# Three fp32r terms for the up products of batches 0 to 5, centred up weights, and a new order of the tail in an RWKV and mixture-of-experts kernel

## What is computed

```python
shifted = pad(hidden)[:, :-1]                       # the token before
key, value, rec = (hidden * m + shifted * (1 - m) for m in (mix_k, mix_v, mix_r))
k, v, r = key @ Wk, value @ Wv, sigmoid(rec @ Wr)
rwkv = _wkv(time_decay, time_first, k, v)           # a scan over time with running max, numerator, denominator
x = layernorm(hidden + r * rwkv @ Wo)
gate = softmax(x @ router_w.T) * top2_mask          # 8 experts
a = silu(einsum('bth,eih->beti', x, down_w))        # 16 hidden units per expert
out = einsum('beth,bte->bth', einsum('beti,ehi->beth', a, up_w), gate)
x = layernorm(x + out)
```

## Time and profile before

| | |
|---|---|
| median of 3 runs | 495.65 us (495.41 to 495.65) |
| the profiled execution | 495.26 us, its span 493.4 us |
| mean granted TensorE clock | 0.986 of full speed |
| busy share of the span | PE 96%, PEld 64%, DVE 83%, ACT 69%, POOL 53% |
| DMA | 29.95 MB on the queue, 18.6% of the 16 engines' span |

### The profile page before, as it was taken

How to read it: one execution, slowest core, us unless ns; L and a number is a source line. 1 busy time by engine, 2 the same in 40 slices (tenths; PEclk the granted TensorE clock), 3 DMA queues, 4 the chain that set the end, 5 groups by cost and what they waited for, 6 DMA issues and landing times. The chain is left out here.

```text
span 493.4 us, 6302 instructions
## 1 busy us (share of the span) xinstructions
PE 471.9 (96%) x1850; PEld 316.4 (64%) x1850; DVE 408.8 (83%) x655; ACT 338.7 (69%) x769; POOL 259.5 (53%) x279
## 2 busy tenths in 40 slices
PE   8998799999999999999999999999999999999991
PEld 3444377777777667775777667776677656776550
DVE  6998988897799878997799977998699977776686
ACT  1568365865867678786777769776787767657574
POOL 2446764566515964457625767259635574321326
PEclk9999799999999999999999999999999999999997
DMA  9800250003000042004110032001320012300015
GB/s 248 277 12 1 86 191 1 0 3 85 1 1 0 24 147 87 1 1 129 64 64 1 1 129 106 22 1 63 107 89 1 0 43 86 128 1 1 1 38 219
DMA packets 20098, 30.35 MB, mean 62 GB/s; under 512 B 2016, under 2 KB 7136, under 8 KB 20064
## 3 DMA queue, kind: packets, MB, share of 16 engines
q1 hardware_dynamic: 20064, 29.95, 18.6%
HBM read 21.56 MB, written 8.39 MB: 61 GB/s over the span
## 5 line engine op out<-in xcount | busy, mean ns | idle before, releaser
L514 ACT ACTIVATE PR<-PR 128x512 f32<-128x512 f32 x128 | 74.3, 581 | 53.0 <-PE PR L296 23.1
L320 PE MATMUL PP<-WO,RW 128*128 128x512 f32 x216 | 97.3, 592 | 0.0
L1026 POOL TENSOR_SCALAR NM<-SUM,RS 128x1 f32<-128x1 f32 x30 | 9.1, 302 | 157.3 <-ACT RS L514 157.3
L320 PEld LDWEIGHTS PP<-WO,RW 128*128 128x128 f32 x216 | 39.5, 190 | 41.3 <-issue 40.9
L1020 POOL TENSOR_TENSOR DQ<-DEN,EX 128x512 f32<-128x512 f32 x32 | 41.0, 1282 | 35.4 <-DVE DEN L730 35.4
L767 DVE TENSOR_TENSOR RW<-NU,PR 128x512 f32<-128x512 f32 x32 | 22.0, 687 | 42.3 <-ACT PR L514 42.2
L778 DVE SCALAR_TENSOR_TENSOR KT<-D,VEC,XT 128x512 f32<-128x512 f32 x56 | 52.0, 959 | 0.0
L292 PE MATMUL PV<-VH,WVH 128*128 128x512 f32 x112 | 47.0, 420 | 0.4 <-DVE NU L754 0.4
L292 PE MATMUL PK<-KH,WKH 128*128 128x512 f32 x112 | 47.2, 422 | 0.0
L730 DVE TENSOR_TENSOR_SCAN DEN<-PK,EX 128x512 f32<-128x512 f32 x32 | 39.1, 1221 | 9.7 <-ACT EX L514 7.5
L292 PE MATMUL PR<-RH,WRH 128*128 128x512 f32 x112 | 47.0, 419 | 0.2 <-DVE RW L767 0.2
(11 more groups left out here) (200 smaller groups left out, 1119.2 us busy)
## 6 DMA issues: line engine op xcount, KB each, us to landing
XT<-in_xt SPq DMA_DIRECT2D x32, 256.0 KB, 3.6
XN<-in_x SPq DMA_DIRECT2D x28, 256.0 KB, 2.7
out<-XN SPq DMA_DIRECT2D x28, 256.0 KB, 2.0
WO<-in_wo SPq DMA_DIRECT2D x1, 1024.0 KB, 7.7
XT<-in_x SPq DMA_DIRECT2D x4, 256.0 KB, 4.1
out<-XT SPq DMA_DIRECT2D x4, 256.0 KB, 2.2
X1T<-in_wk SPq DMA_DIRECT2D x2, 256.0 KB, 4.9
XN<-in_wv SPq DMA_DIRECT2D x2, 256.0 KB, 5.3
```

The lines of the kernel that those rows point to most:

```text
L320: last = eng.matmul(projected_at(t), RW[(C * b + c) % NRW][:, 128 * n:128 * n + 128], WO[:, c, :], start=(c == 0), stop=(c == C - 1))
L514: eng.activation(*a, **k).then_inc(q[s], 1)
L1026: eng.tensor_scalar(NM1[:, col(t)], total, RS1[:, col(t)], scale, ALU.mult, ALU.mult)\
```

## The change

- UP is centred over its 512 columns once (ACT sums a row of it, POOL makes the mean and subtracts it), in slots 4 and 5. The row mean of the second residual is then zero, since its other summand is normalised. So `residual2` no longer makes a sum, `spread2` squares without a bias, `normalise2` loses its 128x1 product and `finish` its subtraction.
- UP is split into UPH and UPL (fp32r). For batches 0 to 5 `ffn_out` writes AGH (fp32r), DVE subtracts it from the turned gates in PSUM to AGL (`gated_low`, new), and `ffn_up` is three fp32r matmuls. Batches 6 and 7 stay fp32.
- SCR (4 x 512 columns) becomes JUNK (512). Batch 0's key mixes go to WO, so WO's load moves behind DR and TRI and waits for the fourth key product.
- The up product of `j = 0` goes behind the projection. In the tail the order of PE, ACT, DVE and POOL changes; MEASURED shrinks from five tiles to three, all of batch 7, FINISHED from two to one, and Ln and Exp of batch 6 are made for two tiles at a time.

```diff
@@ full @@
-                early = [AGT[:, :], UP[:, :]] + ...
-                return (SCR[:, c, :], RW[C + c][:, :], early[c])[which]
+                early = [JUNK[:, :], UP[:, :]] + ...
+                return (WO[:, c, :], RW[C + c][:, :], early[c])[which]
@@
-        MEASURED = [NT * (LAST - 2) + 3, NT * (LAST - 1) + 1, NT * (LAST - 1) + 3, NT * LAST + 1, NT * LAST + 3]
+        MEASURED = [NT * LAST + 1, NT * LAST + 2, NT * LAST + 3]
-        FINISHED = [NT * LAST + 1, NT * LAST + 3]
+        FINISHED = [NT * LAST + 3]
@@ sync @@
-            load_w(WO, wo, "wo")
             load_w(DR, dr, "dr", 0, HD)
             eng.dma_start(TRI[:, :], tri).then_inc(q["tri"], 16)
+            eng.wait_ge(q["k"], C)
+            load_w(WO, wo, "wo")
@@ tensor, ffn_up @@
+                if k < LAST - 1:
+                    eng.wait_ge(q["agl"], k + 1)
...
-                eng.matmul(up_at(t), PARTS[k].agt[:, o:o + 128], UP[:, :],
-                           start=True, stop=True).then_inc(q["up_"], 1)
+                if k < LAST - 1:
+                    eng.matmul(up_at(t), AGH[:, o:o + 128], UPH[:, :], start=True, stop=False)
+                    eng.matmul(up_at(t), AGH[:, o:o + 128], UPL[:, :], start=False, stop=False)
+                    last = eng.matmul(up_at(t), AGL[:, o:o + 128], UPH[:, :], start=False, stop=True)
+                else:
+                    last = eng.matmul(up_at(t), PARTS[k].agt[:, o:o + 128], UP[:, :], start=True, stop=True)
+                last.then_inc(q["up_"], 1)
@@ tensor, the loop @@
-                if j == 0 and batch(b - 3):
-                    ffn_up(t3 + 3)
                 if j == 0:
                     for t in now[:1]:
                         project(t)
+                if j == 0 and batch(b - 3):
+                    ffn_up(t3 + 3)
                 rec(s)
@@ tensor, the tail @@
             turn(t7)
+            ffn_turn(LAST - 1)
+            ffn_up(t5)
             project_most(t7 + 3)
             project_rest(t7 + 3)
             turn(t7 + 1)
             hidden(t7)
+            ffn_up(t5 + 1)
             turn(t7 + 2)
-            ffn_up(t5)
             hidden(t7 + 1)
-            ffn_up(t5 + 1)
+            ffn_up(t5 + 2)
             turn(t7 + 3)
             hidden(t7 + 2)
+            ffn_up(t5 + 3)
             hidden(t7 + 3)
-            ffn_turn(LAST - 1)
-            ffn_up(t5 + 2)
-            ffn_up(t5 + 3)
+            ffn_up(t6)
             ffn_turn(LAST)
-            ffn_up(t6)
@@ scalar @@
+                if s == C:
+                    eng.wait_ge(q["up"], 16)
+                    act("upx", JUNK[:, :], UP[:, :], ACT.Copy, accum_out=SUMU[:, :])
+                if s == C + 1:
+                    eng.wait_ge(q["upc"], 1)
+                    act("uph", UPH[:, :], UP[:, :], ACT.Copy)
@@ vector @@
+            def gated_low(k):
+                eng.wait_ge(q["agc"], k + 1)
+                eng.tensor_tensor(AGL[:, :], PARTS[k].turned_at, AGH[:, :].bitcast(F32), ALU.subtract)\
+                   .then_inc(q["agl"], 1)
@@ vector, the loop: behind scan_max(s + 1) and lead(s + 1), ahead of the mixes @@
+                if j == 2 and s < U - 2 and batch(b - 2):
+                    gated_low(b - 2)
                 if j == 2 and b:
                     mixes(b + 1, 1, 0, 1)
...
                 if s == U - 1:
+                    gated_low(LAST - 2)
                     gate_scores(LAST - 1)
@@ gpsimd @@
             def normalise2(t):
...
-                eng.tensor_scalar(xn_at(t), xn_at(t), RS2[:, col(t)], NM2[:, col(t)], ALU.mult, ALU.add)\
-                   .then_inc(q["nrm2"], 1)
+                eng.tensor_scalar(xn_at(t), xn_at(t), RS2[:, col(t)], None, ALU.mult).then_inc(q["nrm2"], 1)
@@
+                if s == C:
+                    eng.wait_ge(q["upx"], 1)
+                    eng.tensor_scalar(NMU[:, :], SUMU[:, :], -1.0 / H, None, ALU.mult).then_inc(q["upm"], 1)
+                    eng.wait_ge(q["upm"], 1)
+                    eng.tensor_scalar(UP[:, :], UP[:, :], NMU[:, :], None, ALU.add).then_inc(q["upc"], 1)
+                if s == C + 1:
+                    eng.wait_ge(q["uph"], 1)
+                    eng.tensor_tensor(UPL[:, :], UP[:, :], UPH[:, :].bitcast(F32), ALU.subtract).then_inc(q["upl"], 1)
```

More of the change, by code:

```diff
@@ L74, in rwkv_moe_postln @@
         ST, MV = sb("ST", [128, 7, 6]), sb("MV", [128, 7, 2])
-        SUM2, SQ2, LV2, RS2, NM2 = (sb(n + "2", [128, 3 * NT]) for n in ("SUM", "SQ", "LV", "RS", "NM"))
+        SQ2, LV2, RS2 = (sb(n + "2", [128, 3 * NT]) for n in ("SQ", "LV", "RS"))
+        SUMU, NMU = sb("SUMU", [128, 1]), sb("NMU", [128, 1])
         PK = [bank("PK0"), bank("PK1")]
@@ L113, in __init__ @@
                 tail = self.b == LAST
-                x = SCR if tail else X1T
                 hs = spare[:, 0:NT * HD].rearrange("p (n h) -> p n h", n=NT) if tail else HS[self.b % 2]
@@ L117, in __init__ @@
                 gm = spare[:, 768:780].rearrange("p (i n) -> p i n", i=3) if tail else GM
-                self.s1, self.s2 = (x[:, i, EI * lo:EI * hi] for i in range(2))
-                self.gt, self.eq = (x[:, 2 if tail else 1, o + E * E * lo:o + E * E * hi] for o in (0, 256))
+                s1, s2, pairs = (M, DEN, NUM) if tail else (X1T[:, 0, :], X1T[:, 1, :], X1T[:, 1, :])
+                self.s1, self.s2 = (a[:, EI * lo:EI * hi] for a in (s1, s2))
+                self.gt, self.eq = (pairs[:, o + E * E * lo:o + E * E * hi] for o in (0, 256))
                 self.hs = hs[:, lo:hi, :]
@@ L573, in spread, with spread2 @@
                 act("rs1", RS1[:, col(t)], LV1[:, col(t)], ACT.Exp, scale=-0.5)
-            def spread2(t):
+            def spread2(t, n=1):
+                cols = slice(col(t).start, col(t).start + n)
                 if t in MEASURED:
                     i = MEASURED.index(t)
-                    eng.wait_ge(q["mv2"], i + 1)
-                    act("lv2", LV2[:, col(t)], MV[:, i, 1:2], ACT.Ln, bias=EPS)
-                else:
[L581 to L587, removed]
+                    eng.wait_ge(q["mv2"], i + n)
+                    eng.activation(LV2[:, cols], MV[:, i:i + n, 1], ACT.Ln, bias=EPS).then_inc(q["lv2"], n)
+                else:
+                    for u in range(t, t + n):
+                        eng.wait_ge(q["res2"], u + 1)
+                        act("sq2", JUNK[:, :] if u == t else KT[0][:, :], xn_at(u), ACT.Square, accum_out=SQ2[:, col(u)])
+                    eng.wait_ge(q["sq2"], squared(t + n - 1, MEASURED))
+                    eng.activation(LV2[:, cols], SQ2[:, cols], ACT.Ln, bias=EPS, scale=1.0 / H).then_inc(q["lv2"], n)
+                eng.wait_ge(q["lv2"], t + n)
+                eng.activation(RS2[:, cols], LV2[:, cols], ACT.Exp, scale=-0.5).then_inc(q["rs2"], n)
             def turned(t):
@@ L691, in _ @@
             spread(t7 + 2)
+            ffn_out(LAST - 1)
+            spread2(t5)
             turned(t7 + 1)
@@ L696, in _ @@
             hidden_copy(t7 + 1)
-            spread2(t5)
+            ffn_in(LAST)
             turned(t7 + 3)
             hidden_copy(t7 + 2)
-            ffn_in(LAST)
+            spread2(t5 + 1)
             hidden_copy(t7 + 3)
-            ffn_out(LAST - 1)
             ffn_in(LAST + 1)
             ffn_out(LAST)
-            spread2(t5 + 1)
+            spread2(t5 + 2)
             ffn_out(LAST + 1)
-            for t in range(t5 + 2, NT * NB):
+            spread2(t5 + 3)
+            spread2(t6, 2)
+            spread2(t6 + 2, 2)
+            for t in range(t7, NT * NB):
                 spread2(t)
@@ L969, in _ @@
             residual(t7 + 2)
+            residual2(t5)
             residual(t7 + 3)
             moments(t7 + 3)
-            residual2(t5)
+            residual2(t5 + 1)
             gate_scores(LAST)
+            residual2(t5 + 2)
             gate_top(LAST)
-            residual2(t5 + 1)
-            residual2(t5 + 2)
+            silu(LAST)
+            residual2(t5 + 3)
             gate_scores(LAST + 1)
-            silu(LAST)
             gate_top(LAST + 1)
-            residual2(t5 + 3)
             silu(LAST + 1)
[L982 to L987, removed]
+            for n in range(NT):
+                residual2(t6 + n)
             residual2(t7)
-            moments2(t6 + 3)
             residual2(t7 + 1)
@@ L1085, in _ @@
                     normalise2(t2 + 1)
+                if s == C:
[4 more added lines that the diff above has]
+                if s == C + 1:
+                    eng.wait_ge(q["uph"], 1)
+                    eng.tensor_tensor(UPL[:, :], UP[:, :], UPH[:, :].bitcast(F32), ALU.subtract).then_inc(q["upl"], 1)
             t5, t6, t7 = (NT * (LAST - i) for i in (2, 1, 0))
-            for n in range(NT):
+            for n in range(NT - 1):
                 normalise(t7 + n)
-            for t in range(t5, NT * NB):
+            normalise2(t5)
+            normalise(t7 + 3)
+            for t in range(t5 + 1, NT * NB):
                 if t not in FINISHED:
```

38 lines of the change are left out of this document (17 added, 21 removed), and 2 rows, old and new, of the table q.

## The result

The changed kernel takes 498.1 us (median of four runs, 497.8 to 498.4), the kernel before 495.65 us on the same chip: a ratio of 1.005, 95% interval 1.0033 to 1.0068. It is 2.5 us slower, where I had forecast 6.4 us faster, and it lies outside my range.

What follows compares the result with a forecast made beforehand. It took a ring of VectorE and ScalarE, then some TensorE work, to bound the kernel, not TensorE's 96% busy time. Loop 3.4 plus tail 3.0 gave 6.4 us off 495.65: 489.2 us, range 485.5 to 492.8.

Steps and rivals of the forecast that it cites:

- Part 6: Tail: GpSimd's second normalisation needs 0.77 us per tile without the product, so the end comes 3.0 us earlier; bounds 0 to 4.
- B: Rival, tail gives nothing: 492.2 us, 10%; a sign is VectorE or TensorE releasing the last factors.
- Part 4: Smaller edits in the loop, such as the normalisation losing its 128x1 product on GpSimd: nothing gained, taken as 0.
- Part 5: Start: later WO load costs 0; centring and splitting UP costs 0 to 1 us, taken as 0.
- Part 2: Loop: fourth up product behind the projection starts the decay gates 0.69 us earlier, five times, 3.4 us saved.
- Part 3: Loop: gated_low, 0.6 us on VectorE, is covered by the mixes' loss during GpSimd's run; cost 0, bounds 0 to 3.0.
- Part 1: Three fp32r terms for one fp32 up product save TensorE 4.1 us over 24 tiles, worth nothing outside the ring.
- the ring: A batch's loop: some 49.8 us of VectorE and ScalarE, then 7.4 of TensorE; matmul time saved elsewhere gives nothing.
- The period of 56.6: Loop: forecast time per batch after the change, in us, against 57.31 before; a sign that the forecast is right.
- A: Rival: gated_low isn't covered in the loop, 3.0 us less gain, 492.2 us, 17%; its sign a period of 57.2.
- C: Rival: TensorE paces the loop and its whole saving counts, 6.9 us, with the tail 9.9: 485.8 us, 8%.
- D: Rival, slower: an idle gap of TensorE in the tail halves its clock, 499.2 us; 5% with other ways to be slower.

Runs made afterwards that it cites:

- two_ops: The changed kernel, its second normalisation on GpSimd multiplying by the factor and then by 1.0 (two operations, same result): 492.33 us, ratio 0.9927.
- before_one_op: The kernel before, its second normalisation on GpSimd cut to one operation, the mean not subtracted, the 128x1 product still made: 502.59 us, ratio 1.0141.
- keep_small: two_ops with a 128x1 product on GpSimd, into a buffer nobody reads, ahead of each second normalisation: 491.95 us, ratio 0.9929.
- best: start with GpSimd's normalisation in slots j = 3 moved between the second and third receptance subtraction: 488.54 us, ratio 0.9859.
- start: two_ops with UP split earlier in slot 5: high copy ahead of the decay gates, low part right behind GpSimd's denominator: 490.84 us, ratio 0.9897.
- f32_no_low: f32_up with the gated_low subtraction and TensorE's wait for it also taken out: 492.66 us, ratio 0.9931.
- low_twice: best with gated_low's subtraction made twice in each of the five j = 2 slots, result unchanged: 489.37 us, ratio 0.9864.
- f32_up: two_ops with one fp32 up product for the three terms in batches 0 to 5, low part of the gates left out: 492.64 us, ratio 0.994.

## Why the prediction was wrong

**The step that failed is in Part 6**: "Without the product it needs 0.77 per tile". I took the 0.77 from a row of another form, two operations with two scalars per partition, and gave it no bounds, as I did not see the instruction as changed. It measures 1.56. With 1.56 my own tail would have read: GpSimd has five tiles left at 483.2, so it ends at 491.0, 0.9 later than before, not 3.0 earlier. Measured: 2.1 later (37.02 against 34.91), since GpSimd was behind by then and had six left at 483.16. two_ops and before_one_op show the cause from both sides, 5.8 us back and 7.0 us lost. The tail's order, ScalarE's factors and VectorE's end came within half a microsecond of what I wrote (but for ScalarE's wait of 0.47 us for VectorE, one of my signs for B), and with two operations the tail gains 3.4 for my 3.0.

**Part 4, the small edits.** "In the loop GpSimd waits for others, so nothing is gained" looked for a gain only. The slow form costs 0.16 us a batch (14.36 for 14.20, four times), and the missing 128x1 product 0.44, five times: I had seen that GpSimd's work would start 0.6 us earlier, but looked at the third mix and its cover of 2.08, not at the second, which has none. keep_small and best both remove the 0.44.

**Part 5, the start.** 1.17 us, where my bounds were 0 to 1 and I took 0. I let the added GpSimd pass delay "denominators, needed some microseconds later", and left out that the key subtractions behind them block the mixes; start takes it back. WO's later load is seen nowhere: up to weigh 4 the steps agree within 0.15.

**What held.** Part 2: 0.73 per batch for 0.69, five times, with the decay gates released by VectorE's lead. Part 3: gated_low at 0, by f32_no_low, and with the bounded cover I described, by low_twice; it takes 0.60 from start to start (267.67 to 268.27) while GpSimd's four key subtractions run. Part 1: TensorE's time outside the ring is worth 0.3 us of 4.1 at most. The period of 56.6 is there to the digit in keep_small and best (56.58, 56.59). With the three misses repaired the sum stands: five times 0.73 and the tail's 3.4 are 7.1, and best takes 488.5, 7.1 below the kernel before; the forecast was 489.2. That is the kernel I had in mind and not the one I forecast.

**The rivals.** The loop's period came out at 57.2, which I had called the mark of A, but the step A speaks of is unchanged, at 13.36: the period alone told two causes not apart. C falls with f32_up. D didn't come: from 440 to 485 us the granted clock is 1.00, the last up product ends at 482.5, and TensorE's longest pause on the way is 0.38 us (1.02 before). B's "nothing from the tail" was too kind to the change as made. My case of a slower kernel, with 5%, rested on the clock; the real one stood in the diff, so the 5% covered it in name only.

## What to carry to other kernels

An instruction that loses an operand or an operation is a new instruction: if no row shows its form, give it a run of its own before it enters the sum, above all where it is the last in the chain. Bounds from its neighbours would not have done here: the two-operation form takes 0.77 and the engine's product of two tensors 1.28, and the 1.56 lies above both. Where two engines hold each other up in turn, removing a short instruction can take away the turn in which the other got in, and adding work ahead of a run moves the run against the other engine: read both timelines at that place. And one test with a do-nothing second operation, `x * s * 1.0`, was worth 5.8 us.

## What the runs showed of the hardware

- GpSimd, tensor_scalar of 128x512 fp32: 1.50 to 1.57 us with one operation, 0.70 to 0.77 with two. UP's centring, one addition, takes 1.57 as well. I had not expected that less work takes twice the time. The Trainium skill (GPSIMD Engine Reference, Elementwise — side-by-side cycle accounting) gives 769 ns for 512 elements as the best case of a tight loop. The form with two scalars per partition takes just that (0.77), the one with a constant a little less (0.70), and those with one operation twice as long. Why the one is slower, no run here shows.
- A 128x1 instruction between two long ones on GpSimd let a blocked VectorE instruction in 0.4 us earlier (keep_small against two_ops), five times per execution.
- The first weigh of kernels that are alike up to it comes between 26.9 and 27.8 us, so two single traces can differ by 0.9 us before anything has changed; the steps between weighs that nothing has changed agree within 0.05.
